# Sorted tokens as fp16 halves in DRAM, transposed by the DMA instead of TensorE

## The reference

```python
# D = 512, E = 4 experts; Wg = Wu = Wd = ctx (4 x 512 x 512), so each expert has one matrix
x = x + attention(layernorm(x))
h = layernorm(x)
for e in range(E):
    g = silu(einsum('bsd,fd->bsf', h, ctx[e]))
    u = einsum('bsd,fd->bsf', h, ctx[e])
    y = einsum('bsf,df->bsd', g * u, ctx[e])
    out = where(expert_ids == e, y, out)
x = x + out
x = x + ternary_ffn(layernorm(x))
```

## Time and profile before

| | before |
|---|---|
| median of the runs | 766.53 us (764.83, 766.53, 767.41) |
| span of the profiled execution, first to last instruction | 762.1 us |
| what lies around the span, median less span | 4.4 us |
| TensorE busy | 718.1 us (94%) |
| VectorE, ScalarE, GpSimd busy | 388.6, 276.1, 108.5 us |
| mean granted TensorE clock | 0.983 |

### The profile page before, as it was taken

One profiled execution on the slowest core, in us unless ns is written; L12 is line 12 of the kernel. 1 busy time (PEld: TensorE's weight loads), 2 busy tenths in 40 slices (PEclk: granted clock), 3 DMA queues, 4 the chain that ended last, 5 costly groups with the idle time before them and its releaser, 6 DMA issues.

```text
span 762.1 us, 11832 instructions
## 1 busy us (share of the span) xinstructions
PE 718.1 (94%) x3882; PEld 380.7 (50%) x3883; DVE 388.6 (51%) x672; ACT 276.1 (36%) x430; POOL 108.5 (14%) x154
## 2 busy tenths in 40 slices
PE   4999999999996789999994999999999999999997
PEld 2465556566464556555553444444444444444443
DVE  5568666676537855444457343453434434343223
ACT  3465554555454355222224222222222222222221
POOL 4203034033021400000005000000000000000000
PEclk9999999999998999999997999999999999999999
DMA  7983034033044396222212000020000100010001
GB/s 223 391 320 143 1 127 151 0 129 147 1 173 159 130 342 232 78 91 83 83 42 70 27 15 14 14 71 14 15 0 14 69 14 14 0 55 1 0 0 55
DMA packets 32493, 66.73 MB, mean 88 GB/s; under 512 B 6352, under 2 KB 6352, under 8 KB 31440
## 3 DMA queue, kind: packets, MB, share of 16 engines
q1 hardware_dynamic: 28464, 53.24, 20.1%
q0 software_dynamic: 4000, 13.11, 5.0%
HBM read 47.73 MB, written 18.61 MB: 87 GB/s over the span
## 4 chain that ended last, share of the span: by engine, by line
PE 85%; DVE 5%; DMA 3%; issue 2%; ACT 2%; POOL 2%; SPq 1%; DVEq 0%; POOLq 0%; ACTq 0%
PE bank L1056 31%; PE bank L1314 29%; PE bank L1324 14%; PE bank L1049 6%; PE bank L1199 2%; PE bank L1213 1%; DMA nrm<-in_L_ffn_W_down_dram 1%; PE bank L1234 1%; DMA stage<-in_L_attn_Wv_dram 1%; DVE w_att L843 1%; DVE w_att L842 1%; SPq L183 1%; POOL rs L305 1%; DVE st L568 1%; DMA n<-sorted_outputs,pos_now 0%
## 5 line engine op out<-in xcount | busy, mean ns | idle before, releaser
L1314 PE MATMUL bank<-w_att,region 128*128 128x512 f16 (+1 forms) x1024 | 233.1, 381 | 0.8 <-ACT w_att L535 0.8
L1314 PEld LDWEIGHTS bank<-w_att,region 128*128 (+1 forms) x1024 | 100.5, 98 | 120.5 <-issue 3.6
L1022 DVE SCALAR_TENSOR_TENSOR tmp<-tmp,hk,bank 128x512 f32<-128x512 f32 x64 | 47.8, 747 | 153.7 <-PE bank L1314 153.3
L1324 PE MATMUL bank<-region,tmpA 128*128 (+1 forms) x504 | 119.1, 379 | 0.0
L1056 PE MATMUL bank<-w_moe,tmpA 128*128 x456 | 104.6, 379 | 1.5 <-DVE tmpA L913 1.5
L1056 PE MATMUL bank<-xT,w_att 128*128 128x512 f16 x384 | 88.6, 387 | 4.3 <-DVE region L753 2.3
L543 ACT ACTIVATE tmp<-bank,qs 128x512 f32<-128x512 f32 x64 | 44.0, 688 | 125.1 <-PE bank L1314 125.1
L547 ACT ACTIVATE tmpA<-tmp 128x512 f16<-128x512 f32 x64 | 40.4, 631 | 121.7 <-DVE tmp L1022 121.7
L1324 PEld LDWEIGHTS bank<-region,tmpA 128*128 128x128 f16 x504 | 49.2, 98 | 59.6 <-DVE stage L1005 0.9
L1056 PEld LDWEIGHTS bank<-w_moe,tmpA 128*128 128x128 f16 x456 | 44.4, 98 | 47.1 <-issue 1.7
L1025 DVE TENSOR_TENSOR tmpA<-tmp,tmpA 128x512 f16<-128x512 f32 x64 | 44.3, 692 | 45.7 <-ACT tmpA L547 45.7
(11 more groups left out here) (134 smaller groups left out, 752.4 us busy)
## 6 DMA issues: line engine op xcount, KB each, us to landing
stage<-in_L_ffn_W_up_dram SPq DMA_DIRECT2D x8, 1024.0 KB
stage<-in_L_ffn_W_gate_dram SPq DMA_DIRECT2D x8, 1024.0 KB, 7.0
sorted_tokens<-a SPq DMA_DIRECT2D x10, 512.0 KB, 10.3
n<-sorted_tokens SPq DMA_DIRECT2D x20, 256.0 KB, 2.6
stage<-in_ctx_dram SPq DMA_DIRECT2D x4, 1024.0 KB
stage<-in_L_ffn_W_down_dram SPq DMA_DIRECT2D x4, 1024.0 KB
nrm<-in_L_ffn_W_down_dram SPq DMA_DIRECT2D x4, 1024.0 KB, 7.4
out_dram<-stage SPq DMA_DIRECT2D x16, 256.0 KB, 2.1
```

What stands on the lines that cost most here:

```text
L1022: dve.scalar_tensor_tensor(out=h32, in0=sil, scalar=hk[:, 0:1], in1=gate_ps[:, :], op0=ALU.mult, op1=ALU.mult).then_inc(s["hid_mul"], 1)
L1314: mm = pe.matmul(dst, w[:, bass.ds(cf_c, 1), k * P:(k + 1) * P].rearrange("p a n -> p (a n)"), x3T[:, bass.ds(b, 1), i, k].rearrange("p a ...
L1324: mm = pe.matmul(ffy_ps[t][:, :], hid[:, parity, i, t * P:(t + 1) * P], tern[2][:, bass.ds(c, 1)].rearrange("p a n -> p (a n)"), start=(st ...
```

## The change

Second norms are kept as two fp16 numbers for each value, the upper half and the remainder, side by side in one row of the same 2048 bytes. VectorE writes the norm into a scratch buffer (`nrm` in the passes, `tmp` in the tail), casts it to fp16 in `n2`, and subtracts. The scatter sends both halves. The fetch of a sorted tile is a transposing DMA that lands as eight 128 x 128 blocks, ready as the first product's operand. TensorE's transposes, ScalarE's `xs_hi` and VectorE's `xs_lo` are gone. A slot is free when the first product has read it (`z_mm`), not when it has been transposed. 19 tiles are fetched, not 20.

```diff
-    xs_dram = nc.dram_tensor("sorted_tokens", ((SLOTS + 1) * P, D), F32, kind="Internal").ap()
+    xs_dram = nc.dram_tensor("sorted_tokens", ((SLOTS + 1) * P, 2 * D), F16, kind="Internal").ap()
...
         def sorted_tile(i, slot):
-            sp.dma_start(xs_slot[slot], xs_v[:, bass.ds(i, 1)].rearrange("p a d -> p (a d)")).then_inc(
+            sp.dma_start_transpose(out=xs_slot[slot].rearrange("p i k s -> p (i k) s"),
+                                   in_=xs_v[:, bass.ds(i, 1)].rearrange("p a d -> p (a d)")).then_inc(
                 s[f"xs_in{slot}"], 16)
...
         sp.wait_ge(s["t1_mm"], T * B)
+        sp.wait_ge(s["x2_lo"], T * (B - 1))
         unit(0, 2)
...
                 unit(g, j)
-                sp.wait_ge(s["tx_mm"], 3 * (g - 2) + j + 1)
+                sp.wait_ge(s["z_mm"], 3 * (g - 2) + j + 1)
                 sorted_tile(3 * (g - 1) + j, j)
...
-            wait_apart(pool, "x2_norm", T * b + t + 1)
+            wait_apart(pool, "x2_lo", T * b + t + 1)
             pool.indirect_dma_start(xs_dram, bass.IndirectOffsetOnAxis(ap=pos_now[:, t:t + 1], axis=0),
-                                    n2[:, t], None).then_inc(s["scattered"], 16)
+                                    n2h[:, t].rearrange("p i d -> p (i d)"), None).then_inc(s["scattered"], 16)
...
-        def xs_hi(i):
-            act.wait_ge(s["tx_mm"], i + 1)
-            act.wait_ge(s["z_mm"], i)
-            act.activation(xsT[:, 0], tx_ps[:, :], ACT.Copy).then_inc(s["xs_hi"], 1)
...
             dve.wait_ge(s["t1_mm"], T * b1)
+            dve.wait_ge(s["x2_lo"], T * (b1 - 1))
...
+        def second_norm(b, t, n32):
+
+            normalise(2, n32, x_tile(T * b + t), t, "x2_norm")
+
+        def second_halves(b, t, n32):
+            wait_apart(dve, "x2_norm", T * b + t + 1)
+            dve.tensor_copy(n2h[:, t, 0], n32).then_inc(s["x2_hi"], 1)
+            wait_apart(dve, "x2_hi", T * b + t + 1)
+            dve.tensor_tensor(n2h[:, t, 1], n32, n2h[:, t, 0], ALU.subtract).then_inc(s["x2_lo"], 1)
...
+                dve.wait_ge(s["t1_mm"], T * (b + 1))
                 for t in range(T):
-                    second_norm(b - 1, t)
+                    second_norm(b - 1, t, nrm[:, t])
+                for t in range(T):
+                    second_halves(b - 1, t, nrm[:, t])
...
-            second_norm(B - 1, t)
+            if t >= 2:
+                dve.wait_ge(s["x2_lo"], T * (B - 1) + t - 1)
+            second_norm(B - 1, t, tmp[:, t % 2])
+            second_halves(B - 1, t, tmp[:, t % 2])
...
-            pe.wait_ge(s["xs_lo"], i + 1)
+            pe.wait_ge(s[f"xs_in{slot}"], 16 * slot_count)
             pe.wait_ge(s["h_mul"], i)
-            moe(z_ps[:, :], xsT, e).then_inc(s["z_mm"], 1)
-            xs_transpose(i + 1, slot, slot_count)
+            moe(z_ps[:, :], xs_slot[slot], e).then_inc(s["z_mm"], 1)
```

More of the change, by code:

```diff
@@ L134, in decoder @@
     unit_slot = [stage[:, 0], stage[:, 1], nrm[:, :, :]]
-    xs_slot = [n2[:, i] for i in range(3)]
+    n2h = n2[:, :, :].rearrange("p t d -> p (t d)").bitcast(F16).rearrange("p (t i d) -> p t i d", t=T, i=2)
+    zeros = a32[:].rearrange("p a b -> p (a b)").bitcast(F16).rearrange("p (c d) -> p c d", c=2)
+    xs_slot = [n2h[:, i].rearrange("p i d -> p (i d)").rearrange("p (i k s) -> p i k s", i=2, k=K) for i in range(3)]
     ys_slot = [n2[:, 3], a32[:, 0], a32[:, 1]]
@@ L138, in decoder @@
     tA = tmpA[:].rearrange("p a b -> p (a b)").bitcast(F16).rearrange("p (i h n) -> p i h n", i=2, h=2)
-    xsT, hT = tA[:, 0], tA[:, 1]
+    hT = tA[:, 1]
     hid = tA
@@ L144, in decoder @@
     acc, tr, kv_ps, o_ps, prep = ps[0:2], ps[2:4], ps[4], ps[5:7], ps[7]
-    z_ps, y_ps, tx_ps, th_ps, q_ps = ps[0], ps[1], ps[2], ps[3], ps[4:8]
+    z_ps, y_ps, _, th_ps, q_ps = ps[0], ps[1], ps[2], ps[3], ps[4:8]
     ffy_ps, up_ps, gate_ps, t3_ps = ps[0:4], ps[4], ps[5], ps[6]
@@ L208, in weights @@
                 with sp.Fori(0, (SLOTS + 1) // 2) as i:
-                    sp.dma_start(xs_v[:, bass.ds(2 * i, 2)], a32[:, :, :]).then_inc(s["zeroed"], 16)
+                    sp.dma_start(xs_v[:, bass.ds(2 * i, 2)], zeros).then_inc(s["zeroed"], 16)
             else:
@@ L254, in _ @@
             for j in range(3):
-                sp.wait_ge(s["tx_mm"], 3 * g + j + 1)
+                sp.wait_ge(s["z_mm"], 3 * g + j + 1)
                 sorted_tile(3 * g + j + 3, j)
-        for i in (18, 19):
-            sp.wait_ge(s["tx_mm"], i - 2)
-            sorted_tile(i, i % 3)
+        sp.wait_ge(s["z_mm"], 16)
+        sorted_tile(18, 0)
         sp.wait_ge(s["y_evac"], SLOTS)
@@ L913, in tile_step @@
             dve.tensor_tensor(hT[:, 1], th_ps[:, :], hT[:, 0], ALU.subtract).then_inc(s["h_lo"], 1)
-        xs_lo(0)
         signs_of(1, 1)
@@ L1253, in _ @@
             unit_transposes(0, j)
-        def xs_transpose(i, slot, slot_count):
-            pe.wait_ge(s[f"xs_in{slot}"], 16 * slot_count)
-            pe.wait_ge(s["xs_lo"], i)
-            transposes(tx_ps, lambda k: xs_slot[slot][:, k * P:(k + 1) * P]).then_inc(s["tx_mm"], 1)
         def expert(i):
@@ L1264, in moe @@
         def moe(dst, lhs, e):
-            return product(dst, lambda i, j, k: lhs[:, i, k * P:(k + 1) * P],
+            return product(dst, lambda i, j, k: lhs[:, i, k],
                            lambda i, j, k: w_moe[:, bass.ds(e, 1), j, k].rearrange("p a d -> p (a d)"))
@@ L1288, in _ @@
         pe.wait_ge(s["route_ready"], 1)
-        xs_transpose(0, 0, 1)
         unit_transposes(1, 0)
-        tile_step(0, ((1, 1), (1, 2)), 1, 1, True)
+        tile_step(0, ((1, 1), (1, 2)), 0, 1, True)
         for j in range(3):
-            tile_step(j + 1, ((2, j),), (j + 2) % 3, 1 + (j + 2) // 3, False)
+            tile_step(j + 1, ((2, j),), (j + 1) % 3, 1 + (j + 1) // 3, False)
         with pe.Fori(1, 6) as g:
             for j in range(3):
-                tile_step(3 * g + j + 1, (), (j + 2) % 3, g + 1 + (j + 2) // 3, False)
+                tile_step(3 * g + j + 1, (), (j + 1) % 3, g + 1 + (j + 1) // 3, False)
         second(SLOTS - 1)
```

14 lines of the change are left out of this document (3 added, 11 removed).

## The result

| | before | changed |
|---|---|---|
| median of four runs each | 765.68 us (763.25 to 767.41) | 774.0 us (770.92 to 775.6) |
| changed to before | | 1.010, 95% interval 1.0078 to 1.0121 |
| span of the profiled execution | 762.1 us | 774.0 us |
| mean granted TensorE clock | 0.983 | 0.972 |

The changed kernel is 1.0% slower. The forecast was 770.2 us, slower by 3.7 us; it became 8.3 us. The profiled execution of the changed kernel took 775.6 us for a span of 774.0, so 1.6 us lie around a span, not 4.4: the profiled execution of before was about 3 us faster than the median it was set against. The forecast's sum is one of differences, so this does not touch its terms. The two profiled spans differ by 11.9 us, the medians by 8.3: the execution of the changed kernel that was profiled was the slowest of its four, and that of before a quick one.

The account below looks back on a forecast made before the run. TensorE was taken to bound the kernel, with 85% of the chain that ended last. Loop -7.9, passes +6.4, tail +1.9, transposing DMA +1.6 and clock +1.7 gave +3.7 us, so 770.2 us, range 764 to 787.

Parts of the forecast that it names:

- The loop: Expert loop: eighteen tiles each lose 0.44 us of TensorE transposes, -7.9 us; a tile step falls from 6.06 to 5.62 us.
- Hidden work: Expert loop: hidden tile ready in about 1.5 us under a 2.59 us product; slots and units also hidden, no new wait.
- The halves in the passes: Passes 1 and 2: VectorE's added casts and subtractions take 4.3 us, TensorE stalls 3.2 us in each; +6.4 us.
- Pass 3: Last pass: the added 4.3 us fall into 7.48 us in which VectorE waits for kv products; no cost.
- The clock: Behind the new stalls in passes 1 and 2: one fall of TensorE's clock to half speed, +1.7 us (bounds 0 and 6.8).
- The tail: Stretch before the expert loop: added casts and subtractions delay the last scatter and the units behind it; +1.9 us.
- the transposing DMA in the crowd: Before the loop: two transposing fetches ahead of the awaited unit, at twice the plain price on busy DMA engines; +1.6 us.
- The sum: Whole kernel: all terms together +3.7 us, slower, 770.2 us; chance 0.47 for 768.9 to about 788.
- Rival A: Expert loop: transposing DMAs bound it, from 5.6 us a tile on; about +55, 822 us; chance 0.17.
- Rival B: Faster: stall of only 2.7 us a pass, tail delay hidden, clock steady; -2.5, 764.0 us; chance 0.11.
- Rival C: No change: the sum without clock fall and without extra DMA price; +0.4, 766.9 us; chance 0.25.

Follow-up runs that it names:

- first norm first: Changed kernel with VectorE writing the next batch's first norm ahead of the second norm, which follows tile by tile through `tmp`; 766.11 us, ratio 0.9997.
- plain fetch: Changed kernel with a plain DMA of the same bytes in place of the transposing one, so sorted tiles stay untransposed; 769.55 us, ratio 1.0043.
- filler: Changed kernel with 15 unused matmuls on TensorE ahead of the waiting transposes of the first norm in passes 1 and 2; 771.57 us, ratio 1.0061.
- both units first: Changed kernel with SyncE issuing the two units of group 1 ahead of sorted tiles 0, 1 and 2; 769.64 us, ratio 1.0041.

## Why the prediction was right, and where its sizes were off

The sign and the mechanism were right: TensorE sets the pace, the loop gains what the transposes took, and the passes and the tail give back more. By its terms:

- **The loop, -7.9 us.** Right. 18 steps took 114.37 us before and 106.6 to 106.8 in the first experiments that had the clock up at its start (first norm first, plain fetch, filler, both units first): -7.7. In the changed kernel itself it was -6.4, since the clock was down for its first products.
- **Hidden work.** The second product covers the hidden tile, units and slots came in time, and no wait for a tile appears in the loop.
- **The halves in the passes, 4.3 us and a stall of 3.2.** Measured 4.75 and 3.72. The cast took 0.42 us for the 0.44 assumed, but the dependent subtraction starts 0.52 us after it and a pair takes 1.13, not 1.05. The sum of both stalls is 7.4 us, for 6.4. Pass 3: nothing, as predicted.
- **The clock, one fall for 1.7 us.** This term was mis-sized. The rows that bracketed it had a fall after 4.20 us idle and none after 2.09 (the row shows the idle stretch itself; the 8.04 us behind it read 1.00 as well); 3.7 us of idleness brought one in both passes, at 1.6 us each by the filler. A third fall, behind the tail's wait of 3.19 us, cost 1.3 us at the start of the loop, which makes 4.6 us, and 0.5 in the tail, counted there.
- **The tail, 1.9 us, and the transposing DMA in the crowd, 1.6 us.** Together 3.5, measured 5.5. The plain fetch splits it: 1.4 us for the halves and 4.2 us for the transposing fetch, good to about a microsecond. The step that failed: I priced the fetch by its load on the DMA engines alone, and its issue at nothing, though every fetch of SyncE in the rows was a plain one of 0.34 us. It holds the queue for 1.23 us or more, and two stand ahead of the unit that is waited for: 1.9 us. The load on the engines, priced at 1.6, is met by the 1.8 us by which the unit lands slower. The fetches came later than said as well: the last scatter is issued 0.78 us behind the last subtraction's end, the signs' start moved by 4.0 us for the 3.7, and the first fetch by 2.8 for the 2.0. That the halves still cost only 1.4 us comes from the unit's landing, which behind plain fetches is 1.5 us shorter at the later place (7.84 for 9.30); I had not counted on that.
- **The sum.** -7.7 + 7.4 + 4.6 + 5.5 = +9.8 us, against +9.96 for the profiled spans without the 1.9 us ahead of pass 1. Of the 6.1 us missed on these spans 2.9 are the clock, 2.0 the tail with its queue, 1.0 the stalls and 0.2 the loop. On the medians 4.6 us were missed, and the pair of profiled executions does not say which of the terms were smaller there.
- **Rival A** (the fetches bound the loop) falls: 3.3 us to landing against a step of 5.62. Its sum was off too: 57 less 10 with the terms that it names comes to about +59, not +55. **Rival B** needed a stall under 2.8 us; the stall was longer, not shorter. **Rival C** needed a steady clock and a free fetch, and neither came.

On the fetch the Trainium skill (Advanced Engine Details and Errata, X-Bar Transpose (TRN2)) says that it is as fast as a regular one. By the landing the runs agree roughly: 3.3 us against 2.7 of the plain fetch in the kernel that differs only in it. For the queue that issues it they do not: 1.23 us against 0.34. The estimate of 10.5 us a tile, eight times the 1309 ns of the Trainium skill (VectorE: DVE Perf Modes, The three transpose paths), fell with rival A: the eight blocks landed in 3.3 us.

## What to carry over

Work added to an engine with idle time costs by its place, not by its amount: look at what stands behind it in that engine's order and who waits for that, and move what is not urgent behind what is. Here the halves, 4.75 us of VectorE a pass, cost 5.6 us in one place and 1.3 in another. A stall of 3.7 us ahead of TensorE cost 1.6 us more by the clock, so price each stall with its fall. A DMA's price has a part in the queue that issues it and a part in the landing of what stands behind it: put what others wait for ahead of the slow kind, and check that a borrowed buffer or a moved wait doesn't hold up something else, as happened here twice.

## What the runs showed of the hardware

- **A transposing fetch of 256 KB** takes 1.23 to 1.96 us of SyncE's queue in the loop's first steps and up to 4.02 while the DMA engines are crowded, both in the changed kernel; a plain one takes 0.33 to 0.68. A 1 MB unit behind two of them landed in 9.10 to 10.12 us (four profiles), behind two plain ones at the same place in 7.84, behind one transposing fetch, with the unit before it gone earlier, in 7.19. The page of the changed kernel counts more packets and small ones, 49678 in all against 32493, of them 26097 under 512 B against 6352:

```profile
DMA packets 49678, 66.47 MB, mean 86 GB/s; under 512 B 26097, under 2 KB 26097, under 8 KB 48625
```

- **VectorE and GpSimd slow each other** while both work in SBUF. Four head norms, which have one tensor input in SBUF, took 1.91 us alone, 3.03 with part of GpSimd's additions beside them, 5.82 with all. Two products with both inputs in SBUF took 1.29 alone and 3.13 to 3.25 beside the additions, which took 6.30 there and 5.50 otherwise. The Trainium skill (SBUF — State Buffer, SBUF: two separate sides) says that GpSimd contends for one pair of ports with a VectorE instruction in a two-port mode, and with one that has two inputs in SBUF if GpSimd's reads SBUF too, and that the pair is held for a whole instruction. The runs agree in that both kinds slowed, by these numbers; in which mode the head norms ran no trace shows. I had reckoned with the first kind alone when I placed the additions.
- **The clock** fell to the lower level behind every idle stretch of 3.67 to 4.21 us in the passes, at a cost of 1.6 us each where the filler measured it. At the same place about 23 us into the kernel it fell behind idle stretches of 2.27, 2.38, 2.50 and 2.59 us, and stayed up behind ten of 0.96 to 2.18. In the tail it fell behind 3.18 (first norm first) and 3.19 us (changed kernel) and stayed up behind 3.08 (filler). So the length of a stall did not decide alone here.
